# First batch of a Mamba-plus-experts layer: moving two scans, the decayed X and one weight spread

## What is computed

```python
    x = _layernorm(x + _L0_attn_ref(x, ...), axis=-1)
    x = _layernorm(x + _L0_ffn_ref(x, ...), axis=-1)

# the mixer
z, ssm_in = x @ Wz, x @ Win            # B, C, dt, X are column blocks of ssm_in
h = dA[..., None, None] * h + X_t[..., None] * dB[:, :, None, :]   # one step per token
y_t = jnp.einsum('bhpn,bn->bhp', h, C_t)
output = (y + D_param * X) * (silu(z) @ Wzg) @ Wout
# the mixture
dw1, dw2, dw3 = (_route_dense(x @ P_w.T @ U.T, K, TAU) for U in (U1, U2, U3))   # top 3 of 12
h = gelu(_apply_mixture(x, dw1, W1))        # y += x @ W[e].T * dw[:, e:e+1], e < 12
y = _apply_mixture(h, dw2, W2) + dw3 @ b2
```

## Time and profile before

| | us |
|---|---|
| median of 3 runs | 1562.29 |
| lowest and highest | 1562.07, 1563.94 |
| the profiled execution | 1562.6 |
| its span (first to last instruction) | 1560.8 |

### The profile page before, as it was taken

One profiled execution on the slowest core, in us unless ns is written; L12 is line 12 of the kernel. 1 busy time (PEld: TensorE's weight loads), 2 busy tenths in 40 slices (PEclk: granted clock), 3 DMA queues, 4 the chain that ended last, 5 costly groups with the idle time before them and its releaser, 6 DMA issues.

```text
span 1560.8 us, 25335 instructions
## 1 busy us (share of the span) xinstructions
PE 1544.8 (99%) x8646; PEld 1251.1 (80%) x8646; DVE 1114.6 (71%) x3113; ACT 598.7 (38%) x1360; POOL 658.8 (42%) x751
## 2 busy tenths in 40 slices
PE   9999999999999999999999999999999999999998
PEld 7778788888888878888788888878888788887876
DVE  7677676877768687676776768777686776767755
ACT  6643424425144351533425244242443515335130
POOL 6671623616145270643616335162451705436040
PEclk9999999999999999999999999999999999999999
DMA  5340312304022140321403123140230403214020
GB/s 182 99 142 28 118 39 67 98 29 135 16 78 87 29 135 14 103 69 46 119 15 120 45 65 100 28 131 20 72 93 28 137 14 97 74 38 127 15 75 7
DMA packets 81456, 114.53 MB, mean 73 GB/s; under 512 B 10144, under 2 KB 37296, under 8 KB 81328
## 3 DMA queue, kind: packets, MB, share of 16 engines
q1 hardware_dynamic: 81328, 112.92, 24.7%
HBM read 107.76 MB, written 5.13 MB: 72 GB/s over the span
## 4 chain that ended last, share of the span: by engine, by line
PE 92%; POOL 3%; DVE 1%; issue 1%; DMA 1%; ACT 1%; SPq 0%; POOLq 0%; DVEq 0%; ACTq 0%
PE exp_bank L246 22%; PE exp_bank L248 22%; PE exp_bank L247 22%; PE mix_bank L895 4%; PE mix_bank L921 3%; PE mix_bank L246 3%; PE mix_bank L248 3%; PE mix_bank L247 3%; PE mix_bank L903 3%; PE mix_bank L792 1%; PE turn_bank L1248 1%; POOL w_lo L444 1%; PE mix_bank L738 1%; PE mix_bank L1012 1%; PE mix_bank L524 1%
## 5 line engine op out<-in xcount | busy, mean ns | idle before, releaser
L1189 POOL TENSOR_TENSOR sp_lo<-fbuf,sp_hi 128x512 fp32r<-128x512 f32 (+2 forms) x201 | 243.9, 1217 | 182.9 <-ACT sp_hi L1185 112.5
L246 PE MATMUL exp_bank<-w_hi,sp_hi 128*128 128x512 f32 x768 | 307.9, 401 | 0.8 <-POOL sp_lo L1241 0.8
L246 PE MATMUL exp_bank<-sp_hi,w_hi 128*128 128x512 f32 x764 | 304.0, 398 | 0.3
L248 PE MATMUL exp_bank<-w_hi,sp_lo 128*128 128x512 f32 x768 | 303.5, 395 | 0.0
L247 PE MATMUL exp_bank<-w_lo,sp_hi 128*128 128x512 f32 x768 | 303.4, 395 | 0.0
L248 PE MATMUL exp_bank<-sp_hi,w_lo 128*128 128x512 f32 x764 | 300.5, 393 | 0.0
L247 PE MATMUL exp_bank<-sp_lo,w_hi 128*128 128x512 f32 x764 | 298.5, 391 | 0.0
L1288 DVE SCALAR_TENSOR_TENSOR acc<-exp_bank,dw,acc 128x128 f32<-128x128 f32 x384 | 132.2, 344 | 151.9 <-PE exp_bank L248 151.1
L1185 ACT CAST sp_hi<-fbuf 128x512 fp32r<-128x512 f32 (+2 forms) x203 | 120.0, 592 | 280.1 <-DVE fbuf L1155 220.8
L855 POOL TENSOR_TENSOR Wt<-Wt,Gh 128x512 f32<-128x512 f32 x128 | 184.5, 1442 | 24.4 <-DVE Wt L847 24.4
L246 PEld LDWEIGHTS exp_bank<-sp_hi,w_hi 128*128 128x128 f32 x764 | 143.6, 188 | 39.0 <-issue 9.0
(11 more groups left out here) (267 smaller groups left out, 2289.6 us busy)
## 6 DMA issues: line engine op xcount, KB each, us to landing
row_b<-dw_rows SPq DMA_DIRECT2D x189, 256.0 KB, 3.4
seg_b<-dA_rows SPq DMA_DIRECT2D x124, 256.0 KB, 3.6
ctd<-cum_rows SPq DMA_DIRECT2D x128, 96.0 KB, 3.3
x_in<-in_x SPq DMA_DIRECT2D x16, 256.0 KB, 2.8
result<-acc SPq DMA_DIRECT2D x15, 256.0 KB, 2.3
fbuf<-in_W1T SPq DMA_DIRECT2D x12, 256.0 KB, 3.7
acc<-in_W2T SPq DMA_DIRECT2D x5, 256.0 KB, 3.6
x_in<-in_W2T SPq DMA_DIRECT2D x5, 256.0 KB, 3.1
```

Of the source, the lines that this page charges most:

```text
L246: nc.tensor.matmul(ps, s_hi, m_hi, start=start and j == 0, stop=False, skip_group_check=onto)
L248: last = nc.tensor.matmul(ps, s_lo, m_hi, start=False, stop=stop and j == n - 1, skip_group_check=onto)
L1189: sig("xw_lo", on.tensor_tensor(lo[:, cols], wide[e % 2][:, cols], hi[:, cols].bitcast(F32), ALU.subtract))
```

## The change

The stream of POOL: the third last tile of W1 (split 10) is taken before the memset of `b2_sb` and so before the wait on `x1`; the decayed X (L768, L776) is taken behind split 12 instead of behind split 14, without the wait for the second expert's rest (`xw_lo`). The rest of expert 3's input goes from DVE to POOL (`LO_E`), and the product of head 0 stands between the rests of experts 3 and 4. The rows of POOL, from its preparation of batch 1 on, before:

```diff
@@ -377,7 +377,7 @@
                                          ALU.mult, ALU.subtract).then_inc(sems["cast"], 1)
                 DVE.wait_ge(sems["cast"], NCAST)
         NW, RING = 2 * E, 4
-        N1, NHP, LO_V, LO_E, E3 = 12, 2, (0, 1, 2, 3, 22, 23), (2, 3), 4
+        N1, NHP, LO_V, LO_E, E3 = 12, 2, (0, 1, 2, 3, 22, 23), (2,), 4
         late_slot = (0, 1) * 5 + (2, 3)
         late_stage = [acc[:, :, :].rearrange("p c d -> p (c d)"), x_in[:, :, :].rearrange("p c d -> p (c d)"),
                       seg_b[0][:, :], seg_b[1][:, :]]
@@ -771,8 +771,6 @@
                 for c in range(NC - 1):
                     wait(PO, "Xd", b, c + 1)
                     wait(PO, "silu_lo", b)
-                    if b.reg is None and b.off == 1:
-                        wait(PO, "xw_lo", b.prev(), 3)
                     sig("Xde", PO.tensor_tensor(
                         Xde[:, c, :].rearrange("p (h n) -> p h n", h=H), Xd[:, c, :].rearrange("p (h n) -> p h n", h=H),
                         ends[:, c * H:(c + 1) * H].unsqueeze(2).to_broadcast([P, H, HD]), ALU.mult))
@@ -1075,7 +1073,7 @@
                     last = PE.transpose(spread_bank[e][:, tok(c)], dwpad[:, e, c:c + 1].to_broadcast([P, P]), ident[:, :])
                 last.then_inc(sems["spread"], 1)
             if eng is AC:
-                AC.wait_ge(sems["spread"], e + 1)
+                AC.wait_ge(sems["spread"], 2)
                 AC.copy(wide[0], spread_bank[e][:, :]).then_inc(sems["weight0"], 1)
 
         def weigh_hidden(b, hcs):
@@ -1087,7 +1085,7 @@
 
         def weigh_input(b, e):
 
-            DVE.wait_ge(sems["spread"], e + 1)
+            DVE.wait_ge(sems["spread"], e if e == 1 else 3)
             wait(DVE, "dwr", b)
             if e == 2:
                 DVE.wait_ge(sems["scaled"], NH)
@@ -1354,22 +1352,27 @@
                 AC.copy(unit[:, :], ident4[:, :]).then_inc(sems["unit"], 1)
             if not norm_before and eng is DVE:
                 DVE.wait_ge(sems["unit"], 1)
-            if norm_before or eng is not SP:
+            if norm_before:
                 expert_prep(eng, p, 3)
-            if not norm_before:
+                mix_states(eng, b)
+                mix_score_step(eng, b, 0)
+                experts(eng, p, [2], ahead)
+                mix_score_skip(eng, b, 0)
+                mix_decay(eng, b, 0)
+                mix_score_step(eng, b, 1)
+            else:
+                ahead = [6]
+                if eng is not SP:
+                    expert_prep(eng, p, 3)
+                mix_score_skip(eng, b, 0)
+                mix_decay(eng, b, 0)
                 if eng is not SP:
                     expert_prep(eng, p, 4)
-                ahead = [6]
-            mix_states(eng, b)
-            if norm_before or eng is not AC:
-                mix_score_step(eng, b, 0)
-            if not norm_before:
+                mix_states(eng, b)
+                mix_score_skip(eng, b, 1)
                 expert_prep(eng, p, 5)
-            experts(eng, p, [2], ahead)
-            mix_score_skip(eng, b, 0)
-            mix_decay(eng, b, 0)
-            if norm_before or eng is not AC:
-                mix_score_step(eng, b, 1)
+                mix_decay(eng, b, 1)
+                experts(eng, p, [2], ahead)
             e = 3
             late_split = ([], [], [15], [16], [17], [18], [19], [20])
             late_load = ([], [], [], [17], [18], [19], [20], [21])
@@ -1380,8 +1383,9 @@
                 if not norm_before:
                     split_w(eng, late_split[2 * q])
                     load_w(eng, late_load[2 * q])
-                mix_score_skip(eng, b, 2 * q + 1)
-                mix_decay(eng, b, 2 * q + 1)
+                if norm_before or q > 0:
+                    mix_score_skip(eng, b, 2 * q + 1)
+                    mix_decay(eng, b, 2 * q + 1)
                 if q >= 2:
                     mix_from_start(eng, b, q)
                 if q < NQ - 1:
@@ -1508,13 +1512,13 @@
             mix_rates(PE, nxt)
             mix_ends(PE, nxt)
             mix_X(PE, nxt, [2])
-            keep_busy(rb, 8)
+            keep_busy(rb, 11)
             route_transpose(PE, b)
             mix_X(PE, nxt, [3])
             route_logits(PE, b)
             expert_in(PE, b, 0)
             mix_zg(PE, nxt, range(3))
-            for e in range(3):
+            for e in (1, 0, 2):
                 spread_weight(PE, b, e)
             route_rows(PE, b)
             PE.wait_ge(sems["weight0"], 1)
@@ -1623,10 +1627,10 @@
             mix_zg(AC, nxt, range(1))
             route_weights(AC, b)
             mix_zg(AC, nxt, range(1, 3))
-            split_w(AC, [N1 + 2])
             spread_weight(AC, b, 0)
             first_split(AC, b, 1)
             route_rows(AC, b)
+            split_w(AC, [N1 + 2])
             mix_zg(AC, nxt, [3])
             mix_score_step(AC, nxt, 1)
 
@@ -1644,16 +1648,17 @@
                     split_w(PO, [5 + q])
             split_w(PO, [8])
             mix_step(PO, nxt)
-            split_w(PO, [9])
+            split_w(PO, range(9, 11))
             load_b2(PO)
             wait(PO, "x1", b)
-            split_w(PO, range(10, 12))
+            split_w(PO, [11])
             mix_silu_split(PO, nxt)
             wait(PO, "lg", b)
-            split_w(PO, range(N1, N1 + 2))
+            split_w(PO, [N1])
+            mix_ends(PO, nxt)
+            split_w(PO, [N1 + 1])
             PO.wait_ge(sems["dw0"], 1)
             split_w(PO, [N1 + 2])
-            mix_ends(PO, nxt)
 
         def start_sp(b, nxt):
```

## The result

The changed kernel takes **1566.56 us** (median of 8 runs, 1564.82 to 1567.95), the kernel before 1562.43 beside it (8 runs, 1561.4 to 1563.94). The ratio is 1.0026, with a 95% interval of 1.0017 to 1.0035: slower by 4.1 us, where 2.8 were forecast. The time lies in the stated range, near its upper end (1567.0).

The account below looks back on a forecast made before the run. PE was taken as the bound, with the second y product hanging on the row of expert 6. Terms -0.4 + 1.9 + 1.0 + 0.3 = +2.8 us took the median from 1562.3 to 1565.1 us, range 1561.8 to 1567.0.

Parts of the forecast that it names:

- What bounds, and where it is decided: PE's first 120 us: the start of the second y product hangs on the row of expert 6, 10.0 us before it.
- Scans in front of the carries: DVE around the row of expert 6: gain 0, as 1.9 us saved become idle time waiting for ACT's scaling of head 2.
- Weights of expert 1 first: PE's spread of weights: four transposes needed instead of eight, 0.4 us less from `dw0` to the row of expert 2.
- Decayed X: POOL between splits 12 and 13: its pieces hold up DVE's routing operations, a loss of 1.9 us on the routing's end.
- One operation of DVE for one of POOL: DVE's routing: each POOL operation directly following another holds up one DVE operation with two SBUF inputs until it ends.
- More meetings: DVE's two carries and `ctd` product each meet a POOL operation: 1.0 us more, range 0.2 to 1.8.
- Split 10 before the memset: POOL and DVE around x1: L943 and small operations behind it move by -0.3 to +1.3 us, taken as +0.3.
- the rule's -0.3: At L943 on DVE: by the skill's exclusive port lock it goes before the memset or split 10, making the term -0.3.
- The clock, and everything behind y1 rigid: PE from the second y product on: wait some 2.5 us, clock falls as before, everything behind moves rigidly, last wait stays 0.7.
- rival 3: PE's wait before the spread: the clock falls there too, up to 1.3 us more, sum +4.1, 1566.4 us; chance 0.28.
- No collision: Decayed X on POOL: its pieces may not hold DVE, sum +0.1, 1562.4 us; chance 0.22.
- it does what its place suggests: Before the second y product: row of expert 6 or ACT's scaling comes 1.9 us earlier, -3.8, 1558.5 us; chance 0.10.

Follow-up runs that it names:

- second profiled execution: The changed kernel, unaltered, profiled once more: 1567.4 us at a mean clock of 0.997.
- first profiled execution: The changed kernel as first profiled: 1565.21 us at a mean clock of 0.999.
- the nine matmuls: The changed kernel with nine useless matmuls on PE in its wait before the spread of weights: 1564.97 us, ratio 1.0017.

## Why the prediction was right or wrong

**What bounds, and where it is decided.** Right. From 120 us on nothing of the order changed, and the row of expert 6 carried its delay to y1: +2.38 at the row, +2.35 at y1.

**Scans in front of the carries: 0.** Right. The idle time behind the row of 6 is 1.87, forecast 1.9, with the releaser that was named, and ACT's order turned round gave 2.4 us back.

**Weights of expert 1 first: -0.4.** Right in size, by the trace alone, since no run has this part by itself. From the first L1054 to the row of expert 2 it is 5.24 us (74.86 - 69.62), before 5.71 (73.48 - 67.77): -0.5. It holds because the routing is late: with the decayed X taken back the same stretch is 6.27 us (73.39 - 67.12), since the spread then waits for ACT.

**Decayed X: +1.9.** Right, and by its steps: L1042 was put at 68.0 and stands at 68.00. Measured from L1054 to L1054 the routing's end moved by 1.85. In the kernel with this move alone the stretch from the first of these operations to L1054 grew by 2.3 us (6.29 against 4.03), in part on other operations; L1054 itself came 1.80 later, since its x1 was earlier. "One operation of DVE for one of POOL" held for the four operations here and the four there.

**More meetings: +1.0.** Right in sum. From the row of expert 2 to that of 6 it is 12.01 us after and 11.01 before. The size came from where I had put it: the carries took 0.84 and 0.95 (0.42 and 0.96 before) and the `ctd` product 1.38 (0.74 before), which makes 1.05.

**Split 10 before the memset: +0.3.** Mis-sized; it measured 0. L941 took 0.58 instead of 1.08, so it got its turn before the new neighbour, which is what the Trainium skill (SBUF — State Buffer, section "Who interferes with whom") would have it do. But a small operation behind it then took 0.64 against split 10, and x1 was complete at 57.61 as before at 57.62:

```profile
53.97 0.58 DVE L941 TENSOR_SCALAR nrm<-mv 128x4 f32<-128x4 f32 x1
...
55.16 0.64 DVE L960 TENSOR_TENSOR nrm<-nrm 128x4 f32<-128x4 f32 x1
```

Neither the row's +0.3 nor the rule's -0.3 was right for the sum: what one operation was spared, the next one paid.

**The clock, and everything behind y1 rigid.** This is the step that failed. I let the clock fall at y1 "as before" and gave the fall before the spread to rival 3. In most executions it falls at both. The fall at the spread costs 0.84 us at y1, and with it the move of y1 is 3.19 (94.52 to 97.71), where rival 3 had +4.1 on the sum. The second profiled execution is 4.8 us longer than that of the kernel before (1567.4 against 1562.6): 2.35 from the terms of the sum, 0.84 from the clock at the spread, and 0.5 between y1 and the last tiles of W2 (3.69 there), where the wait also grew from 0.72 to 1.01.

That the first profiled execution took 1565.21, where 1565.4 were forecast, is luck: it had no fall of the clock at all, which the forecast had at y1, and it is only 1.46 later than before at the last tiles. What the forecast describes, one fall, at y1, is the profiled execution with the nine matmuls. There the distance is 2.53 at the last tiles and 2.7 over the span, and the sum was +2.8.

The rest, up to the end, is in batches that the change doesn't touch. There the distance from the kernel before grows in steps, by 0.87 and 0.29 in the second profiled execution and by 0.45, 0.57 and 0.18 in the first. The first step is in both in the batch between 403 and 498 us. In the first execution a row of weights landed late there:

```profile
462.43 0.69 DVE L1153 TENSOR_TENSOR fbuf<-turn_bank,row_b 128x512 f32<-128x512 f32 x1 [2.34 <-DMA row_b<-dw_rows]
```

The row before it started at 459.42, and in the kernel before the same pair is 0.99 apart with a wait of 0.31. Nothing points to the change: with the nine matmuls, and the same code in these batches, the distance grows by 0.15 from the last tiles of W2 to the last batch, and it grows in all of the thirteen other profiled executions, by 0.15 to 1.50 us and once by 2.7. The one profiled execution of the kernel before has the least of such steps, so these 1.2 us belong to the comparison of single executions. Why the DMA of a row lands late in some stays open.

**The rivals.** "No collision" and "it does what its place suggests" fell with L1042 at 68.00 and the idle 1.87. The chances for slower and for no change were 0.38 and 0.52; since both the forecast's own mechanism and rival 3's were true together, the kernel ended just over the border between them. The two should have been one case: a wait of 2.5 us was forecast in front of the spread, and a clock that had fallen behind a wait of 2.4 stood in the earlier trace rows.

## What to carry to other kernels

Where POOL worked without gaps here, each small operation of DVE with two inputs in SBUF in a chain beside it took until the end of an operation of POOL, about 1 us for 0.3 of work. Before moving POOL's work beside a chain of small DVE operations, count the pairs. When work is moved out of a chain, look at what the next operation waits for besides it: here the freed 1.9 us became idle time until one instruction of ACT was moved too. And an engine that takes over a step from a busy one also takes over its wait: the rest of tile 18 cost its own 0.7 us on DVE and 3.5 us of standing in front of a tile that had not landed.
